# Selection products of the first layer in two PSUM banks by turns

## The chip, the cores and the metric

One core of a Trainium2 chip. The metric is device time in microseconds (us) of one execution; the kernel before takes 644.46 us, the median of 3 runs (644.11 to 645.67).

## What is computed

Two layers on x of 4 batches x 512 rows x 512 columns. Only the first layer is touched. Cut to it:

```python
xn = _layernorm(x, axis=-1)
s = einsum('bsk,nk->bsn', xn, w_masked) + bias            # 512 x 512 weight, masked by 32 x 32 blocks
inter = xn @ c1_w.T @ c2_w.T                              # rank 16, 1792 columns
idx = argmax(inter.reshape(rows, 56, 32), axis=-1) + arange(0, 1792, 32)
h = relu(einsum('bkm,bm->bk', w1[idx], xn))               # one of each 32 rows of w1 per row of x
g = silu(einsum('bk,bkm->bm', h, w2t[idx]))
x = x + s * g
```

The second layer (attention with one head, and a base weight with experts of low rank) follows on the same rows, with no edit in it.

## The kernel before

A chunk is one batch: 512 rows, in 4 tiles of 128 (`tt`). For each of the 4 chunks of the first layer the kernel computes all 1792 hidden values with dense products, and zeroes those that aren't the first largest of their 32. Products are made of a high and a low part of each operand, three matmuls for one.

The selection: `rank_product` (line 1192) makes the 16 rank values of a chunk in the bank `sel` (bank 6); ACT rounds them (`t_round`, L707) and the DVE takes the rest (`t_rest`, L926). Then for each piece `p` of 512 columns (4 pieces, the last of 256) and each tile `tt`, 16 in all, `select` on PE (L1214) writes 128 rows x 512 columns into `sel`. On the DVE `select_largest` takes the maximum of each 32 columns (`seg_top`, L939) and marks the places equal to it (`eq`, L941), both read out of the bank; `select_count` counts the marks within each 32 by a scan (`counts`, L953), which reads SBUF only. The counts are transposed, in the first chunk by PE (`first_transpose`, L1233, into bank 7), later by a DMA. Where the count is 1 the hidden value stays: `h` (L974). `h` is rounded on ACT (`h_hi`, L779), its rest taken on the DVE (`h_lo`, L983), and both go into the down product.

The order on each engine is written out by hand. On PE the head of a chunk is `rank_product`, then for each tile `s_product` (12 matmuls, L415) and `select(c, 0, tt)`. The body is a loop over 14 tiles `it` of hidden values: the up product of `it` (12 matmuls), the selection product of the next piece, and the down product of `it - 2` (12 matmuls), which waits for `h_lo`. In the first chunk the order is `up_product(0)`, `select(0, 0, 0)`, `up_product(1)`, then the four `s_product`s with `select(0, 0, 1)` to `select(0, 0, 3)` behind the first three; then `select(0, 1, 0)`, and `first_transpose(0)`, which waits for all four scans of piece 0.

The wait of a selection product is on the `eq` of the one before, since both use bank 6:

```python
                if p == 0 and tt == 0:
                    pe.wait_ge(t_split, c + 1)
                else:
                    pe.wait_ge(sel_eq, c * NSEL + p * TT + tt)
```

Each chunk of the DVE goes in the same order: in `body`, for `it` = 0, it does `h`, then `select_largest(c, 1, 0)`, then `h_lo`, then `select_count(c, 1, 0)`. ACT copies each `s_product` out of its bank (`s_read`, L713); in the first chunk it then rounds the next tiles of the weights (`w1_round`, `w2_round`, L723 and L728), and POOL subtracts (`w1_rest`, `w2_rest`, L614 and L619).

Of the kernel before, what the change touches and what calls it, by code (L numbers as in the profile page):

```python
# [18 lines left out]
def block_mask_ffn_then_attention_lora_kernel(  # L19
# [33 lines left out]
    SEG = 32  # L53
    KD = D // P
    TT = S // P
    CH = B
    PIECES = -(-INTER // BANK)
    PW = [min(BANK, INTER - p * BANK) for p in range(PIECES)]
# [17 lines left out]
    with ctx:  # L76
        def sem(name):
            return ctx.enter_context(nc.semaphore(name))
# [112 lines left out]
        t_stack = span_t.take("t_stack", [P, S], F32R)  # L191
# [18 lines left out]
        banks = [ctx.enter_context(nc.psum_tensor(f"bank{i}", [P, BANK], F32)) for i in range(8)]  # L210
# [57 lines left out]
        sel_eq = sem("sel_eq")  # L268
# [131 lines left out]
        def rows(tt):  # L400
            return slice(tt * P, (tt + 1) * P)

        def opens(c):

            return isinstance(c, int) and c == 0

        def s_bank(c, tt):

            return acc[tt] if isinstance(c, int) and c == 0 else up[tt % 2]

        def three(dst, pairs, start=True, stop=True):

            mms = [(a, b) for ah, al, bh, bl in pairs for a, b in ((ah, bh), (ah, bl), (al, bh))]
            for n, (a, b) in enumerate(mms):
                last = nc.tensor.matmul(dst, a, b, start=(start and n == 0), stop=(stop and n == len(mms) - 1))  # L415
            return last
# [7 lines left out]
        up = [banks[0], banks[1]]  # L424
        acc = [banks[2 + tt] for tt in range(TT)]
        sel = banks[6]
        mask_bank = banks[5]
        first_bank = banks[7][:].bitcast(BF16)[:, 0:S]
        first_counts = [counts, first[:, 1]]
        NSEL = PIECES * TT  # L430
# [450 lines left out]
        def _(dve):  # L881
# [47 lines left out]
            def select(c, p, tt):  # L929

                select_largest(c, p, tt)
                select_count(c, p, tt)

            def select_largest(c, p, tt):
                n = p * TT + tt
                segs = PW[p] // SEG
                got = sel[:, 0:PW[p]].rearrange("p (s n) -> p s n", n=SEG)
                dve.wait_ge(sel_done, c * NSEL + n + 1)
                nc.vector.reduce_max(seg_top[:, 0:segs], got, AX.X).then_inc(seg_max, 1)  # L939
                dve.wait_ge(seg_max, c * NSEL + n + 1)  # L940
                nc.vector.tensor_tensor(eq[:, 0:PW[p]].rearrange("p (s n) -> p s n", n=SEG), got,  # L941
                                        seg_top[:, 0:segs, None].to_broadcast([P, segs, SEG]),
                                        ALU.is_equal).then_inc(sel_eq, 1)
# [17 lines left out]
            def body(c, last):  # L961
                for it in range(IT):
                    if 0 < it < 4 * (PIECES - 1):
                        select(c, it // 4 + 1, it % 4)
                    dve.wait_ge(relu_done, c * IT + it + 1)
                    if opens(c):
                        dve.wait_ge(first_tr, it + 1)
                        which = first_bank
                    else:
                        if it % 4 == 0:  # L970
                            for tt in range(TT):
                                dve.wait_ge(ld_first[tt], (c * PIECES + it // 4 + 1) * 16)
                        which = first[:, it // 4 % 2, it % 4, :]
                    nc.vector.scalar_tensor_tensor(h[:], which, 1.0, h[:], ALU.is_equal, ALU.mult).then_inc(h_masked, 1)  # L974
                    if IT - 8 <= it < IT - 4:
                        rows_stats(dve, c + 1, it - (IT - 8))
                    if it == IT - 4:
                        dve.wait_ge(stats_in, (c + 1) * TT + TT)
                    if it == 0:

                        select_largest(c, 1, 0)
                    dve.wait_ge(h_hi_done, c * IT + it + 1)
                    nc.vector.tensor_tensor(h_lo[:, it % 2, :], h[:], h_hi[:, it % 2, :].bitcast(F32),  # L983
                                            ALU.subtract).then_inc(h_split, 1)
                    if it == 0:
                        select_count(c, 1, 0)
                    if it == IT - 4:
                        rows_moments()
                    if it == IT - 2:
                        rows_norm(dve, c + 1)  # L990
# [18 lines left out]
            for k in range(KD):  # L1009
                dve.wait_ge(ws_hi_done, k + 1)  # L1010
                nc.vector.tensor_tensor(ws_lo[:, k, :], ws_raw[:, k, :], ws_hi[:, k, :].bitcast(F32),
                                        ALU.subtract).then_inc(ws_split, 1)
            select_largest(0, 0, 0)
            c2_rest(1)
            select_count(0, 0, 0)
# [170 lines left out]
        def _(pe):  # L1186
# [9 lines left out]
            def s_product(c, tt, early=False):  # L1196

                if not early and tt >= 2:
                    pe.wait_ge(s0_read, c * TT + tt - 1)
                for k in range(KD):  # L1200
                    if early and tt == 0:
                        pe.wait_ge(ws_split, k + 1)
                    last = three(s_bank(c, tt)[:], [(xT_hi[:, k, rows(tt)], xT_lo[:, k, rows(tt)], ws_hi[:, k, :], ws_lo[:, k, :])],
                                 start=(k == 0), stop=(k == KD - 1))
                last.then_inc(s0_done, 1)

            def select(c, p, tt):


                if p == 0 and tt == 0:  # L1210
                    pe.wait_ge(t_split, c + 1)
                else:
                    pe.wait_ge(sel_eq, c * NSEL + p * TT + tt)
                nc.tensor.matmul(sel[:, 0:PW[p]], t_stack[:, rows(tt)],  # L1214
                                 c2_stack[:, p * BANK:p * BANK + PW[p]], start=True, stop=True).then_inc(sel_done, 1)

            def up_product(c, it, early=False):

                if it >= 2:
                    pe.wait_ge(relu_done, c * IT + it - 1)  # L1220
                elif not early:
                    pe.wait_ge(s0_read, c * TT + TT - 1 + it)
                pe.wait_ge(w1_lo, it + 1)
                three(up[it % 2][:], [(w1_hi_t[:, it, k, :], w1_lo_t[:, it, k, :], xT_hi[:, k, :], xT_lo[:, k, :])
                                      for k in range(KD)]).then_inc(up_done, 1)
# [10 lines left out]
            def down_product(it, tts):  # L1236

                pe.wait_ge(w2_lo, it + 1)
                for tt in tts:
                    last = three(acc[tt][:], [(h_hi[:, it % 2, rows(tt)], h_lo[:, it % 2, rows(tt)],  # L1240
                                               w2_hi_t[:, it, :], w2_lo_t[:, it, :])], start=(it == 0), stop=(it == IT - 1))
                return last

            def head(c):
                pe.wait_ge(xT_done, c * TT + TT)
                rank_product()
                for tt in range(TT):
                    s_product(c, tt)
                    select(c, 0, tt)

            def body(c, first):
                if not first:
                    up_product(c, 0)


                for it in range(1, IT + 1):
                    if it < IT:
                        if not (first and it == 1):
                            up_product(c, it)
                        if (it - 1) // 4 + 1 < PIECES:  # L1260
                            select(c, (it - 1) // 4 + 1, (it - 1) % 4)
                    else:
                        pe.wait_ge(relu_done, c * IT + IT - 1)
                        transpose_rows(pe, c + 1, 0)
                    if first:
                        first_transpose(it - 1)
                    if it >= 2:
                        pe.wait_ge(h_split, c * IT + it - 1)
                        if first and it == 2:
                            pe.wait_ge(s0_read, TT)  # L1270
                        down_product(it - 2, range(TT)).then_inc(down_done, 1)
                pe.wait_ge(relu_done, c * IT + IT)
                transpose_rows(pe, c + 1, 1)
                pe.wait_ge(xT_done, (c + 1) * TT + 1)
                transpose_rows(pe, c + 1, 2)
                pe.wait_ge(h_split, c * IT + IT)
                down_product(IT - 1, range(0, 2))
                pe.wait_ge(xT_done, (c + 1) * TT + 2)
                transpose_rows(pe, c + 1, 3)
                down_product(IT - 1, range(2, TT)).then_inc(down_done, 1)  # L1280
# [237 lines left out]
```

## Time and profile before

| what | value |
|---|---|
| median of 3 runs | 644.46 us (644.11 to 645.67) |
| profiled execution | 643.79 us, its span 642.0 us |
| PE busy | 627.1 us, 98% of the span |
| PE weight loads | 503.9 us, 78% |
| DVE busy | 443.0 us, 69% |
| ACT busy | 213.1 us, 33% |
| POOL busy | 245.1 us, 38% |

One execution is profiled; all rows below are of it, and the times in them count from the start of the span. A matmul of 512 columns is shown as 0.39 us long and the next starts about 0.23 us later, since they are pipelined. Line numbers are those of the kernel before. Busy shares are averages; the stalls and the chain are read from the timeline.

### The profile page before, as it was taken

To read this page: it belongs to the slowest core of one execution; us is meant where nothing else is said; L and a number is where in the kernel's file an instruction comes from. 1 tells how busy PE (TensorE), PEld (TensorE's weight loads), DVE (VectorE), ACT (ScalarE), POOL (GpSimd) and SP (SyncE) were. 2 spreads that over 40 slices of the span, in tenths; PEclk is the share of its full clock that TensorE was granted. 3 is DMA by queue.
4 is the path that set the end of the run, shared out by engine and by line. 5 is a ranking of instruction groups with operands and counts; after the bars stand their busy time and mean duration, and the time that the engine had idled before them with its cause. 6 is when DMAs were issued, how large, how long until landed. Compare 5 with 4: busy or idle time off the path is not lost.

```text
span 642.0 us, 8382 instructions
## 1 busy us (share of the span) xinstructions
PE 627.1 (98%) x2910; PEld 503.9 (78%) x2910; DVE 443.0 (69%) x706; ACT 213.1 (33%) x379; POOL 245.1 (38%) x184
## 2 busy tenths in 40 slices
PE   7999999999999999999999999999999999999997
PEld 3768787878888878888878887787877778787886
DVE  7987776687766786766787786676468447745654
ACT  3533432412222312222313243652245134414521
POOL 1455545560000560000550454477316530832353
PEclk9999999999999999999999999999999999999999
DMA  8950000021500021400052722271226034300701
GB/s 247 402 200 1 2 0 1 10 91 33 155 17 9 17 91 29 151 16 8 25 141 45 234 82 75 83 182 67 66 84 182 16 114 102 96 33 34 199 17 51
DMA packets 47311, 54.68 MB, mean 85 GB/s; under 512 B 25648, under 2 KB 26032, under 8 KB 46640
## 3 DMA queue, kind: packets, MB, share of 16 engines
q1 hardware_dynamic: 47280, 54.28, 28.2%
q8 instruction: 18, 0.29, 0.2%
q14 instruction: 13, 0.11, 0.1%
HBM read 40.24 MB, written 8.52 MB: 76 GB/s over the span
## 4 chain that ended last, share of the span: by engine, by line
PE 62%; issue 16%; DVE 11%; POOL 8%; ACT 1%; DMA 1%; POOLq 0%; DVEq 0%; ACTq 0%; SPq 0%
PE bank L415 56%; POOL prod_lo L692 4%; DVE counts L953 3%; POOL g_tile L391 2%; DVE seg_top L939 2%; PE bank L345 2%; POOL g_tile L395 2%; DVE eq L941 2%; PE bank L1214 1%; DMA first<-counts 1%; PE bank L1192 1%; DVE h_lo L983 1%; DVE h L974 1%; POOL rstd L379 1%; DVE ws_raw L1007 1%
## 5 line engine op out<-in xcount | busy, mean ns | idle before, releaser
L415 PE MATMUL bank<-w_hi_t,h_hi 128*128 128x512 f32 x224 | 90.3, 403 | 0.3
L779 ACT ACTIVATE h_hi<-h 128x512 fp32r<-128x512 f32 x56 | 35.4, 632 | 162.8 <-DVE h L974 162.8
L415 PE MATMUL bank<-w_lo_t,h_hi 128*128 128x512 f32 x224 | 87.6, 391 | 0.0
L415 PE MATMUL bank<-xT_hi,w_hi_t 128*128 128x512 f32 x224 | 87.3, 390 | 0.0
L415 PE MATMUL bank<-w_hi_t,h_lo 128*128 128x512 f32 x224 | 87.3, 390 | 0.0
L415 PE MATMUL bank<-xT_hi,w_lo_t 128*128 128x512 f32 x224 | 87.2, 389 | 0.0
L415 PE MATMUL bank<-xT_lo,w_hi_t 128*128 128x512 f32 x224 | 87.2, 389 | 0.0
L391 POOL TENSOR_TENSOR g_tile<-g_tile,s_tile 128x512 f32<-128x512 f32 x31 | 45.7, 1473 | 107.9 <-DVE g_tile L1103 57.3
L953 DVE TENSOR_TENSOR_SCAN counts<-restart,eq 128x512 bf16<-128x512 bf16 (+1 forms) x56 | 74.2, 1326 | 2.4
L939 DVE TENSOR_REDUCE seg_top<-bank 128x16 f32<-128x512 f32 (+1 forms) x64 | 39.5, 618 | 47.3 <-PE bank L1214 47.3
L692 POOL TENSOR_TENSOR prod_lo<-prod,prod_hi 128x512 fp32r<-128x512 f32 x32 | 51.2, 1636 | 31.5 <-ACT prod_hi L819 31.5
L377 POOL TENSOR_TENSOR rstd<-mean_var,eps 128x4 f32<-128x4 f32 x8 | 1.6, 203 | 152.7 <-DVE mean_var L371 152.7
L983 DVE TENSOR_TENSOR h_lo<-h,h_hi 128x512 fp32r<-128x512 f32 x56 | 41.2, 736 | 27.0 <-ACT h_hi L779 25.4
L415 PE MATMUL bank<-b_hi,prod_hi 128*128 128x512 f32 (+1 forms) x136 | 52.4, 385 | 2.0 <-POOL prod_lo L692 1.8
L758 ACT ACTIVATE h<-bank 128x512 f32<-128x512 f32 x56 | 33.5, 598 | 55.5 <-DVE h_lo L983 46.5
L415 PE MATMUL bank<-b_lo,prod_hi 128*128 128x512 f32 (+1 forms) x136 | 51.3, 377 | 0.0
L415 PE MATMUL bank<-b_hi,prod_lo 128*128 128x512 f32 (+1 forms) x136 | 51.3, 377 | 0.0
L415 PEld LDWEIGHTS bank<-w_hi_t,h_hi 128*128 128x128 f32 x224 | 42.1, 188 | 10.0 <-DVE h_lo L983 1.5
L415 PEld LDWEIGHTS bank<-w_hi_t,h_lo 128*128 128x128 f32 x224 | 42.1, 188 | 9.4
L415 PEld LDWEIGHTS bank<-xT_hi,w_lo_t 128*128 128x128 f32 x224 | 42.0, 188 | 8.8
L415 PEld LDWEIGHTS bank<-xT_lo,w_hi_t 128*128 128x128 f32 x224 | 42.1, 188 | 8.7
L415 PEld LDWEIGHTS bank<-xT_hi,w_hi_t 128*128 128x128 f32 x224 | 42.1, 188 | 8.7
(183 smaller groups left out, 1278.0 us busy)
## 6 DMA issues: line engine op xcount, KB each, us to landing
prod<-expert_weights SPq DMA_DIRECT2D x32, 256.0 KB, 5.6
w_raw<-in_w SPq DMA_DIRECT2D x28, 256.0 KB, 9.5
x_res<-in_x SPq DMA_DIRECT2D x4, 1024.0 KB, 8.5
mid_state<-g_tile SPq DMA_DIRECT2D x16, 256.0 KB, 2.1
x_tile<-mid_state SPq DMA_DIRECT2D x4, 1024.0 KB, 5.6
x_res<-mid_state SPq DMA_DIRECT2D x4, 1024.0 KB, 8.2
out<-g_tile SPq DMA_DIRECT2D x15, 256.0 KB, 2.0
x_tile<-in_x SPq DMA_DIRECT2D x3, 1024.0 KB, 5.8
```

Source lines behind the costliest of these rows:

```text
L345: last = nc.tensor.transpose(rows_bank(g, tt)[:, k * P:(k + 1) * P], x_tile[:, tt, k * P:(k + 1) * P], ident[:])
L379: nc.gpsimd.tensor_tensor(rstd[:], rstd[:], neg_half[:], ALU.pow).then_inc(rstd_step, 1)
L391: nc.gpsimd.tensor_tensor(g_tile[:, tt, :], g_tile[:, tt, :], s_tile[:, tt, :], ALU.mult).then_inc(s_free, 1)
L395: nc.gpsimd.tensor_tensor(g_tile[:, tt, :], g_tile[:, tt, :], x_res[:, tt, :], ALU.add).then_inc(rows_done, 1)
L415: last = nc.tensor.matmul(dst, a, b, start=(start and n == 0), stop=(stop and n == len(mms) - 1))
L692: nc.gpsimd.tensor_tensor(prod_lo[:, kt, :], prod[:, kt, :], prod_hi[:, kt, :].bitcast(F32), ALU.subtract).then_inc(prod_split, 1)
L758: nc.scalar.activation(h[:], up[it % 2][:], ACT.Relu).then_inc(relu_done, 1)
L779: nc.scalar.activation(h_hi[:, it % 2, :], h[:], ACT.Copy).then_inc(h_hi_done, 1)
L939: nc.vector.reduce_max(seg_top[:, 0:segs], got, AX.X).then_inc(seg_max, 1)
L941: nc.vector.tensor_tensor(eq[:, 0:PW[p]].rearrange("p (s n) -> p s n", n=SEG), got, seg_top[:, 0:segs, None].to_broadcast([P, segs, SEG]), ...
L953: nc.vector.tensor_tensor_scan(kept[:, tt, 0:PW[p]], restart[:, 0:PW[p]], eq[:, 0:PW[p]], 0.0, ALU.mult, ALU.add).then_inc(sel_count, 1)
L983: nc.vector.tensor_tensor(h_lo[:, it % 2, :], h[:], h_hi[:, it % 2, :].bitcast(F32), ALU.subtract).then_inc(h_split, 1)
```

## The change

The selection products of odd tiles go to bank 7 (`more_sel`), those of even tiles stay in bank 6. This holds for all pieces of chunks 1 to 3, and for piece 0 of chunk 0; in the later pieces of chunk 0 all stay in bank 6, since bank 7 then holds the transposed counts. `sel_bank` names the bank for PE and for the DVE. With two banks a product waits for the `eq` of the product before the last (`n - 1`), and the product `n` = 1 for none.

```diff
+        def sel_bank(c, p, tt):
+
+            return more_sel if tt % 2 and not (opens(c) and p) else sel
...
         sel = banks[6]
+        more_sel = banks[7]
...
             def select_largest(c, p, tt):
                 n = p * TT + tt
                 segs = PW[p] // SEG
-                got = sel[:, 0:PW[p]].rearrange("p (s n) -> p s n", n=SEG)
+                got = sel_bank(c, p, tt)[:, 0:PW[p]].rearrange("p (s n) -> p s n", n=SEG)
...
             def select(c, p, tt):
-                if p == 0 and tt == 0:
+                n = p * TT + tt
+                if n == 0:
                     pe.wait_ge(t_split, c + 1)
-                else:
-                    pe.wait_ge(sel_eq, c * NSEL + p * TT + tt)
-                nc.tensor.matmul(sel[:, 0:PW[p]], t_stack[:, rows(tt)],
+                elif opens(c) and p:
+                    pe.wait_ge(sel_eq, c * NSEL + n)
+                elif n > 1:
+                    pe.wait_ge(sel_eq, c * NSEL + n - 1)
+                nc.tensor.matmul(sel_bank(c, p, tt)[:, 0:PW[p]], t_stack[:, rows(tt)],
                                  c2_stack[:, p * BANK:p * BANK + PW[p]], start=True, stop=True).then_inc(sel_done, 1)
```

No instruction of PE or the DVE is moved against another. The places at which PE's bank or wait differ look like this one, the product of tile 3 in the opening of the first chunk, before:

```order
82 L415 MATMUL bank4<-ws_lo_83,xT_hi_75 128x512
83 L415 MATMUL bank4<-ws_hi_81,xT_lo_76 128x512
84 L1214 MATMUL bank6<-c2_stack_114,t_stack_115 128x512 [waits sel_eq]
85 L415 MATMUL bank5<-ws_hi_81,xT_hi_75 128x512
86 L415 MATMUL bank5<-ws_lo_83,xT_hi_75 128x512
```

and with the change:

```order
82 L419 MATMUL bank4<-ws_lo_83,xT_hi_75 128x512
83 L419 MATMUL bank4<-ws_hi_81,xT_lo_76 128x512
84 L1222 MATMUL bank7<-c2_stack_114,t_stack_115 128x512 [waits sel_eq]
85 L419 MATMUL bank5<-ws_hi_81,xT_hi_75 128x512
86 L419 MATMUL bank5<-ws_lo_83,xT_hi_75 128x512
```

The bank is another, the place between the `s_product`s is the same, and the count that `sel_eq` has to reach is lower by one.

## Rows read from the trace of the kernel before

**Rows 1.** The page: busy time by engine, and the chain by engine

```profile
PE 627.1 (98%) x2910; PEld 503.9 (78%) x2910; DVE 443.0 (69%) x706; ACT 213.1 (33%) x379; POOL 245.1 (38%) x184
...
PE 62%; issue 16%; DVE 11%; POOL 8%; ACT 1%; DMA 1%; POOLq 0%; DVEq 0%; ACTq 0%; SPq 0%
```

**Rows 2.** Line L1214, whom it waits for, who waits for it; then view of waits

```profile
  DVE eq L941: 9.0, 12
...
  DVE seg_top L939: 47.3, 46
...
PE bank L1214 <- DVE eq L941: 3.3, 6, 0.8
```

**Rows 3.** Timeline, opening of chunk 0: start us, us, engine line op, [idle before <-releaser]

```profile
23.57 0.40 PE L415 MATMUL bank<-ws_hi,xT_hi 128*128 128x512 f32 x1
...
26.10 0.39 PE L415 MATMUL bank<-ws_hi,xT_lo 128*128 128x512 f32 x1
26.54 0.50 PE L1214 MATMUL bank<-c_stack,t_stack 128*128 128x512 f32 x1
...
29.87 0.69 DVE L941 TENSOR_TENSOR eq<-bank,seg_top 128x512 bf16<-128x512 f32 x1
...
30.62 0.50 PE L1214 MATMUL bank<-c_stack,t_stack 128*128 128x512 f32 x1 [0.84 <-DVE eq L941]
...
36.86 0.39 PE L415 MATMUL bank<-ws_hi,xT_lo 128*128 128x512 f32 x1
37.29 0.60 ACT L713 ACTIVATE s_tile<-bank 128x512 f32<-128x512 f32 x1 [2.79 <-PE bank L415]
...
37.51 0.47 PE L1214 MATMUL bank<-c_stack,t_stack 128*128 128x512 f32 x1 [0.26 <-DVE eq L941]
...
38.67 0.40 PE L1233 MATMUL bank<-ident_bf,counts 128*128 128x128 bf16 x4 [0.70 <-DVE counts L953]
```

**Rows 4.** The chain that ended last, window 33 to 43 us: start, us, what

```profile
36.05 0.59 DVE seg_top L939
...
36.67 0.70 DVE eq L941
...
37.39 1.23 DVE counts L953
...
39.07 2.82 PE bank L415 x12
```

**Rows 5.** Timeline, head and start of the body of chunk 2

```profile
224.67 0.39 PE L1214 MATMUL bank<-c_stack,t_stack 128*128 128x512 f32 x1
...
236.00 0.39 PE L415 MATMUL bank<-xT_hi,w_lo_t 128*128 128x512 f32 x1
...
236.98 0.68 DVE L983 TENSOR_TENSOR h_lo<-h,h_hi 128x512 fp32r<-128x512 f32 x1
237.12 0.50 PE L1214 MATMUL bank<-c_stack,t_stack 128*128 128x512 f32 x1 [0.72 <-DVE eq L941]
...
237.71 0.50 PE L415 MATMUL bank<-w_hi_t,h_hi 128*128 128x512 f32 x1
```

**Rows 6.** Timeline, POOL and the scan on the DVE, 30 to 39 us

```profile
30.29 1.28 POOL L619 TENSOR_TENSOR w_lo_t<-w_raw,w_hi_t 128x512 fp32r<-128x512 f32 x1
30.60 2.05 DVE L953 TENSOR_TENSOR_SCAN counts<-restart,eq 128x512 bf16<-128x512 bf16 x1
...
31.53 2.20 POOL L614 TENSOR_TENSOR w_lo_t<-w_raw,w_hi_t 128x512 fp32r<-128x512 f32 x1
...
38.48 1.28 POOL L614 TENSOR_TENSOR w_lo_t<-w_raw,w_hi_t 128x512 fp32r<-128x512 f32 x1 [3.51 <-ACT w_hi_t L723]
```

**Rows 7.** Timeline of PE, start of the program: warming matmuls, then the first transposes

```profile
1.65 8.72 PE L1285 MATMUL bank<-restart 128*128 128x512 bf16 x28 [1.65 <-DVE restart L886]
...
6.74 3.62 PE L1285 MATMUL bank<-restart 128*128 128x512 bf16 x16
...
11.23 0.52 PE L345 MATMUL bank<-ident,x_tile 128*128 128x128 f32 x3 [0.87 <-DVE x_tile L385]
```

## The prediction

> **What bounds the kernel now.** I read the page first, for the engines and the chain [rows 1]. PE is busy 627.1 of 642.0 us and PE rows are 62% of the chain that ended last: only what lies in PE's own stalls, or moves PE's start, can change the time. The stalls that the diff speaks of are in the view of the selection's line [rows 2]: in front of the 64 products of `select` PE and its weight loads stand idle 9.0 us, 12 times, for the DVE's `eq`, and the view of waits puts 3.3 us of that, 6 times, on the matmul side. The other products find their wait met or nearly so. The same view says that the DVE waits for these products 46 times, 47.3 us; that is idle time of an engine that is busy 69%, and costs nothing by itself.
>
> A stall removed is a gain only where the next thing PE needs is not late as well, so each of the places is followed in the timeline. There are two kinds.
>
> **Place 1, the opening (26 to 39 us).** PE runs four products of the first weight, 12 matmuls each, with a selection product behind the first three [rows 3]. Its stalls show at 26.54 (the row before starts at 26.10 and the pace is 0.23, so 0.2 us), at 30.62 (0.84 idle) and a small one before the third; then come 37.51 (0.26) and the transposes at 38.67 (0.70, for `counts`). What they wait for is one chain on the DVE without a hole: the windowed chain of work [rows 4] goes maximum, `eq`, scan, each on the DVE and each right behind the one before, and only from 39.07 on is it mostly PE. So the DVE doesn't wait there for a selection product.
>
> **Place 2, the first two tiles of the next piece, once in each of the later three chunks.** The example is the third chunk [rows 5]. The product at 237.12 stood 0.72 idle for `eq`. The next matmul, at 237.71, belongs to the down product and waits for `h_lo`, which runs 236.98 to 237.66. This pair stands three times, with the same gap. In the head of a chunk the products come behind 12 matmuls each and find `eq` finished, as the one at 224.67, with no idle time in its row.
>
> **The change, part by part.**
>
> *Bank and waits.* No instruction is added, and the order on PE and DVE stays. Odd tiles write and are read from bank 7; reads of a bank cost the same by anything that I see (the DVE's maximum and `eq` come out of PSUM either way). One wait per chunk goes, that of the product `n` = 1; the others ask for one `eq` less: tiles 2 and 3 in the opening, and all from the second chunk on. The 12 selection products of the later pieces of the first chunk keep bank 6 and their wait, since bank 7 holds the transposed counts there. One of them, the product at 37.51, still waits for the `eq` of 36.67.
>
> *Waits that were met.* Heads and bodies of chunks 2 to 4: 48 products less the 3 of place 2. Nothing: PE's order puts them behind 12 or 24 other matmuls.
>
> *Place 2, 3 stalls.* The up product issues its last matmul at 236.00, so the selection product can go at 236.23, 0.89 earlier. But the down product still needs `h_lo`, whose DVE chain (`h`, maximum, `eq`, `h_lo`) contains nothing that waits for this product. It starts at 237.71 as before. 3 x 0 = 0. The cover is `h_lo`; without it each stall would return up to 237.71 - 236.46 = 1.25 us at most, and that is the bound for the range.
>
> *Place 1, PE.* From 23.57 on PE now runs without a stop: 4 x 12 matmuls and 3 selection products, so the last one starts 50 steps later. The step is (26.10 - 23.57) / 11 = 0.23, which gives 35.07 instead of 36.86 [rows 3]: 1.79 us earlier. The two waits that are left there are met: the second selection (about 29.3) needs the `eq` that had ended when 26.54 began, the third (about 32.3) the one of 29.87 + 0.69 = 30.56 [rows 3]. Then PE stands before the product at 37.51, since the `eq` of 36.67 ends when it did, and before the transposes, which want all four scans. So the 1.79 us turn into one longer wait, worth 0.
>
> *Place 1, what the earlier PE triggers.* The last copy out of PSUM on ACT (37.29) waits for PE; behind it on ACT stands the rounding of the next weight, and behind that POOL's subtraction at 38.48 [rows 3, 6]. All move 1.79 earlier: the copy to 35.50, POOL to 36.69. It then runs to 36.69 + 1.28 = 37.97, and lies across 37.39, where the DVE wants to start its fourth scan. The rows show what that costs [rows 6]: a scan that starts inside a POOL operation is stretched until 1.08 us after that operation's end: POOL 30.29 + 1.28 = 31.57, the scan of 30.60 ends at 32.65. The POOL operation behind it is stretched in its turn (31.53, 2.20 instead of 1.28). The fourth scan ran alone, in 1.22: 37.39 to 38.61 [rows 4]. Changed it ends at 37.97 + 1.08 = 39.05, 0.44 later. PE's transposes wait for it (0.70 of idle time at 38.67), and from there PE is the chain without a hole: [rows 4] shows the 12 matmuls at 39.07, and PE holds the chain in the same way for the rest of the chunk, 11 stretches of 24 matmuls. So **0.44 us are added**.
> The Trainium skill (GPSIMD Engine Reference, section 1, Specifications) says that GpSimd shares its SBUF interfaces with VectorE, with contention for DVE instructions with two SBUF inputs. The scan has two, and the rows above agree.
>
> *Sum.* 0 + 0 + 0.44 = 0.44 on the profiled execution of 643.79 us (span 642.0), so 644.2. That execution is 0.67 below the median, and the forecast for the median is 644.46 + 0.44, about **644.9 us**. Bounds of the unknown terms: the scan loses nothing if POOL comes after 37.39 (0), and almost a whole POOL operation if POOL starts just before it, 1.28 - (1.22 - 1.08) = 1.14. Place 2 lies between -3 x 1.25 and 0; I take 0, since `h_lo` is measured as the last.
>
> **Rivals.**
>
> *A: no effect at all* (20%). POOL is not early enough, or takes its turn in another way; then the time is 644.5. Against: 0.7 us of margin between 36.69 and 37.39.
>
> *B: the removed stalls are worth their time* (3%). If PE's stalls were on the path, 1.79 in the opening and 3 x 0.6 (237.71 - 237.12 for the selection product that fills the gap) would return, 3.6 us: 640.9, faster by 0.6%. For it speaks the 9.0 us of idle time; against it, that in both places another DVE result ends after the stall.
>
> *C: PE's clock falls in the longer hole* (4%). Waits that were spread are put together: PE would be idle from about 35.3 to 37.51, runs one product, and is idle again to 39.1. Of the 28 warming matmuls at the start of the program the first 12 took 6.74 - 1.65 = 5.09 us and the last 16 took 3.62 [rows 7]; with 0.2 taken off for the last one's own end that is 0.42 against 0.21 each, so I read the first as run at the lower of the two levels, 1.2 GHz. All took 8.72, where 28 x 0.214 + 0.2 = 6.2 would do: a spell at the lower level costs 2.5 us. With the 0.44 this gives 647.4, slower by 0.46%. It decides if the hole is long enough for the throttle. Against: the matmuls kept the upper pace over holes of 0.87 [rows 7] and 0.84 us [rows 3], though these are shorter than 2.2.
> The Trainium skill (TensorE: Matmul & The Clock Gate, Part 1) says that the gate halves the clock after idle time; by it the hole would cost those 2.5 us if it counts as idle. No row of this trace has a hole so long.
>
> *D: POOL gets two turns before the scan* (4%). The scan would wait for the second subtraction as well, 1.28 more: 646.2. Against: the POOL operation at 31.53 waited behind the scan that was already due [rows 6].
>
> *E: the change does not act*, because a wait for the old bank survives. The order of PE shows bank 7 and the missing wait, so this has no chance of its own beyond A.
>
> **The numbers.** Forecast 69%, A 20%, B 3%, C 4%, D 4%. Forecast and A lie within 0.3%, about what a measurement of this kernel can tell from no change (1.9 us, 642.5 to 646.4); so does D. Same 0.93, slower 0.04, faster 0.03. The three runs before spread over 644.11 to 645.67, and the median may move with them. The range takes A from below (644.5 less 0.5), the bound of the scan (644.46 + 1.14), and half a microsecond of spread: 644.0 to 646.1, which leaves out B, C and a part of D.
>
> **What the profile afterwards would show.** Right: the first four selection products at about 20.6, 26.3, 29.3 and 32.3; the last matmul of the fourth product at 35.1; POOL's subtraction near 36.7; the fourth scan about 1.66 long; PE's transposes at about 39.1; in the later chunks the product about 0.9 before its old place and the down product exactly on it. Wrong: a fourth scan of 1.22 (A), transposes before 38.6 or a down product that starts earlier after `h_lo` (B), matmuls of the first up product paced at over 0.4 us (C).

## The result, and the profile after

The changed kernel takes 648.23 us, the median of 6 runs (646.91 to 649.05), against 644.83 us (644.11 to 645.67, 6 runs) for the kernel before, measured together. The ratio is 1.0049, with a 95% interval of 1.0035 to 1.0063: slower by half a per cent, outside the predicted range of 644.0 to 646.1. It is the case that the prediction called C. All six runs have a mean granted clock of TensorE of 0.992 to 0.996. The profiled execution took 649.05 us, its span is 647.2.

The page of the changed kernel, busy times, the granted clock in 40 slices, and the chain by engine:

```profile
PE 629.5 (97%) x2910; PEld 507.0 (78%) x2910; DVE 445.8 (69%) x706; ACT 213.1 (33%) x379; POOL 244.1 (38%) x184
...
PEclk9979999999999999999999999999999999999999
...
PE 61%; issue 16%; DVE 12%; POOL 8%; ACT 1%; DMA 1%; POOLq 0%; DVEq 0%; ACTq 0%; SPq 0%
```

Against [rows 1] the shares hardly move, and a reader of the busy times would see nothing. One digit of the clock says where to look: slice 3 of 40, 32 to 48 us. The changed kernel's stretches there (us, PE busy and count, granted clock, DMA share, GB/s):

```profile
36.00:37.00 1.00, 0.00 (x0) 1.00 1.06 408
37.00:38.00 1.00, 0.66 (x1) 0.65 1.05 408
38.00:39.00 1.00, 0.08 (x1) 0.50 1.05 410
...
43.00:44.00 1.00, 1.00 (x4) 0.50 0.00 0
44.00:45.00 1.00, 1.00 (x8) 0.94 0.00 0
```

The clock falls from its upper level (2.4 GHz) to 0.50 of it (1.2 GHz) and comes back at about 44.1. The row of 37 to 38 us, 0.65, puts the fall at 37.3: 0.3 us at the upper level and 0.7 at the lower. PE's timeline over the same place, which answers to [rows 3]:

```profile
34.90 0.39 PE L419 MATMUL bank<-ws_hi,xT_lo 128*128 128x512 f32 x1
37.18 0.66 PE L1222 MATMUL bank<-c_stack,t_stack 128*128 128x512 f32 x1 [1.89 <-DVE eq L946]
38.92 0.61 PE L1241 MATMUL bank<-ident_bf,counts 128*128 128x128 bf16 x4 [1.09 <-DVE counts L958]
...
39.87 0.63 PE L419 MATMUL bank<-xT_lo,w_hi_t 128*128 128x512 f32 x1
40.29 0.63 PE L419 MATMUL bank<-xT_hi,w_lo_t 128*128 128x512 f32 x1
```

PE got through the opening as forecast, then had nothing for 1.89 us, one product, and nothing for 1.09. I call such idle time a hole, and a stretch at the lower level a spell. The clock fell 0.1 us into that one product, so behind the first hole and before the second. From the product on the matmuls take longer, and behind the second hole they start every 0.42 us instead of 0.23. The DVE, ACT and POOL beside it, which answer to [rows 4, 6]:

```profile
35.33 0.60 ACT L718 ACTIVATE s_tile<-bank 128x512 f32<-128x512 f32 x1 [2.35 <-PE bank L419]
...
36.52 1.27 POOL L619 TENSOR_TENSOR w_lo_t<-w_raw,w_hi_t 128x512 fp32r<-128x512 f32 x1 [1.88 <-ACT w_hi_t L728]
...
37.06 1.80 DVE L958 TENSOR_TENSOR_SCAN counts<-restart,eq 128x512 bf16<-128x512 bf16 x1
```

The fourth scan is 1.80 us instead of 1.22: POOL ends at 37.79, and the scan 1.07 later. A second spell stands in the head of the third chunk. The chain of the changed kernel, in order of time (start, us, what):

```profile
121.11 2.12 PE bank L1197 x8
...
144.62 5.73 PE bank L419 x24
...
216.76 2.12 PE bank L1197 x8
...
241.29 7.38 PE bank L419 x24
...
338.60 5.74 PE bank L419 x24
```

24 matmuls take 7.38 us at 241.29, and 5.73 in the second and last chunks; the granted clock falls there at 242.1, 0.8 us behind the hole. PE's timeline in front of it, and the scan in that head that made its hole longer:

```profile
238.90 0.39 PE L1222 MATMUL bank<-c_stack,t_stack 128*128 128x512 f32 x1
241.29 0.50 PE L419 MATMUL bank<-w_hi_t,h_hi 128*128 128x512 f32 x1 [2.00 <-DVE h_lo L988]
...
223.42 2.37 DVE L958 TENSOR_TENSOR_SCAN counts<-restart,eq 128x512 bf16<-128x512 bf16 x1
223.42 1.29 POOL L391 TENSOR_TENSOR g_tile<-g_tile,s_tile 128x512 f32<-128x512 f32 x1
```

In the kernel before, the same two rows were these; the scan began 0.03 us ahead of POOL, and POOL was the one stretched:

```profile
220.75 1.22 DVE L953 TENSOR_TENSOR_SCAN counts<-restart,eq 128x512 bf16<-128x512 bf16 x1
220.78 2.28 POOL L391 TENSOR_TENSOR g_tile<-g_tile,s_tile 128x512 f32<-128x512 f32 x1
```

The account of the 5.2 us between the two profiled spans closes on four terms, read at the start of each chunk's rank product (before: 118.47, 214.11, 309.80; after: 121.11, 216.76, 314.99) and at PE's transposes and down products:

| term | us |
|---|---|
| fourth scan longer, 1.80 - 1.22 (the DVE's chain itself began 0.33 earlier in this run) | 0.58 - 0.33 = 0.25 |
| transposes to second rank product, 82.19 against 79.80: first spell | 2.39 |
| third head, rank to down product, 24.53 against 23.60: met scan | 0.93 |
| down product to last rank product, 73.70 against 72.09: second spell | 1.61 |
| sum | 5.18 |

The first and third rows together are 1.2, the two spells 4.0. The profiled run is the slowest of the six; how the 3.4 us between the medians divide in the other five isn't shown. The third row is not of the change: it is a race that one or the other kernel can lose. `open_only` below, whose later chunks are as before, lost it as well (2.36 us, a head of 24.52). But there the old waits split PE's idle time in front of the down product, and the clock stayed at 1.00.

### The profile page after: what moved, and what is told of

The parts are those of the page before. It is cut to its first block, busy times and chain, and to the rows that moved or that the text cites. A ratio compares the mean times of both kernels' runs of the same rounds, so it can differ in the third digit from the quotient of the medians.

```text
span 647.2 us, 8380 instructions
## 1 busy us (share of the span) xinstructions
PE 629.5 (97%) x2910; PEld 507.0 (78%) x2910; DVE 445.8 (69%) x706; ACT 213.1 (33%) x379; POOL 244.1 (38%) x184
## 4 chain that ended last, share of the span: by engine, by line
PE 61%; issue 16%; DVE 12%; POOL 8%; ACT 1%; DMA 1%; POOLq 0%; DVEq 0%; ACTq 0%; SPq 0%
PE bank L419 56%; POOL prod_lo L697 4%; DVE counts L958 3%; POOL g_tile L391 2%; DVE seg_top L944 2%; DVE eq L946 2%; POOL g_tile L395 2%; PE bank L345 1%; PE bank L1222 1%; DMA first<-counts 1%; PE bank L1197 1%; DVE h_lo L988 1%; DVE h L979 1%; POOL rstd L379 1%; PE bank L1241 1%
## 5 line engine op out<-in xcount | busy, mean ns | idle before, releaser
L391 POOL TENSOR_TENSOR g_tile<-g_tile,s_tile 128x512 f32<-128x512 f32 x31 | 43.7, 1411 | 108.0 <-DVE g_tile L1108 57.4
L958 DVE TENSOR_TENSOR_SCAN counts<-restart,eq 128x512 bf16<-128x512 bf16 (+1 forms) x56 | 75.6, 1350 | 2.4
```

The source lines that it names most:

```text
L391: nc.gpsimd.tensor_tensor(g_tile[:, tt, :], g_tile[:, tt, :], s_tile[:, tt, :], ALU.mult).then_inc(s_free, 1)
L958: nc.vector.tensor_tensor_scan(kept[:, tt, 0:PW[p]], restart[:, 0:PW[p]], eq[:, 0:PW[p]], 0.0, ALU.mult, ALU.add).then_inc(sel_count, 1)
```

## The experiments

Theory 1 from here on: the change doesn't make PE wait less, it puts PE's idle time together, and the clock falls there; the stretched scan is a small second term. The rivals are that the later chunks carry the loss, that the second bank costs something by itself, and that POOL and the scan are the whole of it. "Clock" below is the mean granted clock of a run; it doesn't say where a spell was. In the 111 runs of the kernel before that were made beside these experiments it was 0.996 twice and never lower, and 0.997 or less in 15. The edits are shown against the changed kernel; those of versions with one bank are the same against the kernel before.

**The opening alone.** Only piece 0 of the first chunk uses two banks.

```diff
-            return more_sel if tt % 2 and not (opens(c) and p) else sel
+            return more_sel if tt % 2 and opens(c) and not p else sel
...
-                elif opens(c) and p:
+                elif p or not opens(c):
```

> Only piece 0 of the first chunk uses two banks; the later chunks are as before. Theory 1 (the hole of PE in the opening, 2.3 us and then 1.5 us with one product between, takes the granted clock down to its lower level, and a scan meets a POOL operation): slower by nearly all of the whole change, 2.5 to 3.5 us, the first up product behind the hole shown at 0.50 of the clock in most runs. Theory 2 (the later chunks carry it): within 0.5 us of before.

648.15 us (644.98 to 650.46, 4 runs) against 644.49; ratio 1.0066 (1.0045 to 1.0086). Three runs have a clock of 0.991 or 0.992 and take 647.7 to 650.5. The fourth, 0.998, takes 645.0, and it is the profiled one: its fourth scan is 1.79 us, its holes are 1.90 and 1.26 us, its clock stays at 1.00 all the same, and its first down product starts as early as in a kernel without a spell (42.40, for 42.17 and the 0.25 of the scan). The opening carries the loss, and in most runs the clock is low, not in all. The slowest run is 6.0 us over before, more than one spell of 2.4 us; what else it had isn't shown.

**The later chunks alone.**

```diff
-            return more_sel if tt % 2 and not (opens(c) and p) else sel
+            return more_sel if tt % 2 and not opens(c) else sel
...
-                elif opens(c) and p:
+                elif opens(c):
```

> Only the later chunks use two banks; the opening is as before. Theory 1: within 0.5 us of before, with now and then a spell of lower clock in one head (1.7 us, as the third chunk of the changed kernel shows). Theory 2: slower by 1.7 us or more in most runs.

645.44 us (644.13 to 648.93, 10 runs); ratio 1.0016 (1.0000 to 1.0033). Eight of the ten lie at 644.1 to 646.2; the other two have clocks of 0.994 and 0.995 and take 648.9 and 647.2. In the profiled run, 646.0, the third head again has a scan of 2.34 us, a hole of 1.98 us in front of the down product, and 24 matmuls in 7.36 us. So heads have spells now and then: a smaller, rarer part.

**Two banks, old waits.**

```diff
-                elif opens(c) and p:
+                else:
                     pe.wait_ge(sel_eq, c * NSEL + n)
-                elif n > 1:
-                    pe.wait_ge(sel_eq, c * NSEL + n - 1)
```

> The two banks, with the waits of the kernel before. Theory 1 (only when PE runs matters): the kernel before, within 0.5 us, granted clock 1.0 in the opening. Rival (reading or writing the second bank costs something by itself): slower by 1 us or more, with longer maxima or eq on the DVE.

644.45 us (643.60 to 644.60, 10 runs), ratio 0.9993 (0.9983 to 1.0003). The bank costs nothing that can be measured. Of the change only the lower counts in the waits are left as a cause, that is, when PE runs.

**PE kept busy in the opening's holes**, by matmuls whose result nobody reads.

```diff
+                        if first and it == 1:
+                            pe.wait_ge(relu_done, 1)
+                            fill(up[0], 8)
                         if (it - 1) // 4 + 1 < PIECES:
                             select(c, (it - 1) // 4 + 1, (it - 1) % 4)
+                        if first and it == 1:
+                            fill(up[0], 6)
```

> The changed kernel with 8 matmuls without use in front of, and 6 behind, the selection product at 37 us, into bank 0, so that PE is busy through the hole. Theory 1: the clock stays at 1.0 in the opening; what is left over before is the stretched fourth scan, 0.3 to 0.5 us, and spells in the heads of some runs, so 0.3 to 1.5 us over before instead of 3.4. If the loss comes from the scan and POOL alone: no change against the changed kernel.

647.41 us (646.50 to 649.48, 5 runs); ratio 1.0046 (1.0029 to 1.0064). The clock stays at 1.00 in the opening as expected, but the time is 2.9 over before, more than I allowed. The profiled run, 647.41, has its loss in the last chunk, where the DVE waited 4.34 us for the transposes by DMA and PE stood 2.85 us. Stretches of it (as above):

```profile
335.00:338.00 3.00, 2.50 (x6) 0.55 0.76 294
338.00:340.00 2.00, 2.00 (x9) 0.82 0.25 57
```

So one can have a clean opening and lose in a head. Of this run's 3.6 us, 1.8 are the head that ended later (the down product 25.36 us behind the rank product, for 23.59), and 1.5 the spell (24 matmuls in 7.21 us for 5.74). The late transposes are thus a loss of their own, and another run, with a clock of 1.0, takes 646.50: 2.0 us over before, with no spell to be seen. Why this version loses that, and why the next one, with the same 14 matmuls in the opening, doesn't, stays open.

**PE kept busy in every hole**: as before, and 5 such matmuls (`fill(acc[0], 5)`) behind the second selection product of the next piece in each later chunk.

> The changed kernel with matmuls without use in every hole that it makes: 8 and 6 about the product at 37 us, and 5 behind the second selection product of the next piece in each later chunk. Theory 1 (spells of lower clock behind the holes are most of the loss, and heads too have them where a scan lost the race against POOL): mean granted clock 0.999 or more in nearly all runs, and 0.5 to 1.0 us over before. Rival (the loss in the heads is POOL's and the scans' alone): no better than the kernel with the opening filled, 2.5 us over before.

645.42 us (644.16 to 646.20, 10 runs) against 644.73; ratio 1.0006 (0.9996 to 1.0016). Clocks 0.999 or 1.0 in nine of ten. What is left over before, 0.7 us in the medians, is about the stretched fourth scan (1.73 us in its profile, 0.5 more than alone), but the interval doesn't tell it from nothing. The 29 matmuls without use, 14 in the opening and 5 in each of three later chunks, take away the loss of the change: the loss was PE's idleness, not its work.

**Only the first hole of the opening left empty** (`fill(up[0], 0)` in place of 8).

> As fill_all, but the first hole of the opening (35.1 to 37.1 us, the one that the change makes) is left empty; behind the product at 37 us 6 matmuls run. If the spell needs the long run of idleness with only one product in it: no spell, as fill_all. If the 2 us alone are enough: clock at 0.50 behind it, 2 to 3 us over fill_all in most runs.

645.33 us (644.07 to 648.01, 10 runs); ratio 1.0014 (0.9996 to 1.0033). Seven runs lie at 644.1 to 646.5; the others are 646.9, 647.9 and 648.0, with clocks of 0.997, 0.995 and 0.997. The profiled run, 644.5, has a hole of 1.90 us at 37.41 and no spell. So with only the first hole left the clock is low (0.997 or less) in three runs of ten, and with both in three of four of `open_only` and in all six of the changed kernel, though these have unfilled heads as well. The second hole thus counts in some runs; but in the profiled run of the changed kernel the clock fell before it, and how it counts isn't shown.

**The stretched scan taken away, the hole left.** One more wait on POOL in the opening:

```diff
+                if it == 4:
+                    gp.wait_ge(sel_count, TT)
```

> The changed kernel with one wait more on POOL: its subtraction that met the fourth scan waits for that scan. The scan is 1.22 us again and PE's transposes 0.6 us earlier. If the spell of lower clock in the opening comes from the hole that the change makes (35.1 to 37.1 us) and the one behind it, now 1.3 instead of 1.9 us: fewer spells, 1 to 3 us over before in the runs that have them and within 0.3 us in the rest. If the scan's 0.6 us were the whole price: before, within 0.3 us, in every run.

645.74 us (644.07 to 649.06, 10 runs) against 643.92; ratio 1.0033 (1.0015 to 1.0051). The fourth scan is 1.22 us. The run with a clock of 1.0 takes 644.07, which is the kernel before; the six from 0.990 to 0.996 take 645.7 to 649.1, and the three of 0.997 take 645.1 to 645.6. The two terms are apart: the scan 0.6 us, the spells the rest. In the profiled run the holes are 2.00 and 0.70 us, and the clock falls at about 39.4, behind the second, for a shorter time:

```profile
38.00:40.00 2.00, 1.30 (x9) 0.86 0.96 374
40.00:42.00 2.00, 2.00 (x6) 0.50 0.17 65
42.00:44.00 2.00, 2.00 (x11) 0.79 0.00 0
```

**Can the holes themselves go?** What makes them is a DVE chain whose scans meet POOL. First try, on both kernels: in the opening POOL's subtractions after the fourth scan, in the later heads the bias additions after the fourth scan.

```diff
-            gp.wait_ge(c2_split, 2)
-            for it in range(2, IT + 2):
+            gp.wait_ge(ws_split, KD)
+            w1_rest(2)
+            gp.wait_ge(sel_count, TT)
+            w2_rest(0)
+            for it in range(3, IT + 2):
...
             def head(c):
+                if not opens(c):
+                    gp.wait_ge(sel_count, c * NSEL + TT)
```

> The kernel before (one bank), with POOL's subtractions of the opening moved off the first four scans and its bias additions behind the fourth scan of each later head. If a scan that starts inside a POOL operation loses what the rows show (0.83 us each) and the DVE's chain sets PE's start there: the opening is 1.7 us shorter (two scans), each of three heads 0.85 (one scan), 642.2 to 640.2 in all, faster by 2.3 to 4.3 us. If something else holds PE: no change.

> The same on the changed kernel (two banks). PE's hole in the opening shrinks from 2 + 1.5 us to about 0.6 + 1.1 and in the heads from 1.25 to 0.4, so theory 1 expects no spells of lower clock and the same time as the one-bank version within 0.5 us. If the two banks cost something apart from the holes: slower than the one-bank version by over 1 us.

Not faster, either of them: 646.18 us (ratio 1.0010, 0.9998 to 1.0021) and 646.14 (1.0016, 1.0002 to 1.0031), against 644.73. The opening did get shorter, PE's transposes are at 36.91 (one bank) instead of 38.67. But POOL's queue was now behind, and met the scans of the next piece and `h_lo`, which reads two tensors of SBUF as well. The chain of the one-bank version:

```profile
43.63 0.04 DVE first L958
43.67 1.95 issue
45.62 0.67 DVE h L979
...
46.98 1.58 DVE h_lo L988
...
48.61 7.32 PE bank L415 x24
```

The first two scans of the next piece, at 39.98 and 43.63, take 2.31 and 2.07 us instead of 1.22 (the second lies under the 1.95 us of "issue" in this view), `h_lo` takes 1.58 instead of 0.69, and PE's hole behind it, 1.79 us, brings a spell with one bank too: 7.32 us for 24 matmuls, for 5.55 before. The two-bank version has the same hole of 1.79 us there and no spell in its profile. So a spell comes behind a hole, whatever makes it, and not each time.

**POOL between the scans.** While the DVE does the maximum and `eq` out of PSUM (1.4 us), a POOL operation of 1.3 us fits.

```diff
-            gp.wait_ge(c2_split, 2)
-            for it in range(2, IT + 2):
+            gp.wait_ge(ws_split, KD)
+            w1_rest(2)
+            gp.wait_ge(sel_count, 1)
+            w2_rest(0)
+            gp.wait_ge(sel_count, 2)
+            w1_rest(3)
+            gp.wait_ge(sel_count, 3)
+            w2_rest(1)
+            gp.wait_ge(sel_count, 4)
+            for it in range(4, IT + 2):
```

> The kernel before (one bank) with POOL's four subtractions of the opening put between the scans, where the DVE reads PSUM (one behind the high and low parts of the first weight, three each behind a scan). The scans are 1.22 us instead of 2.05: transposes at 37.0 instead of 38.7, and unlike with the late subtractions no queue behind them, so faster by 1.4 to 1.7 us. If POOL's work is late for the first chunk again: no gain.

> The changed kernel with POOL's four subtractions of the opening between the scans. PE's hole in the opening is then 0.6 + 1.1 us at most, the heads keep their whole hole behind the selection product (1.25 us, 2.1 where the first scan lost against POOL). Theory 1 (the clock falls where the change puts idle time together): no spell in the opening; spells left in the heads, so between the one-bank version of the same (642.7) and 1.7 us over it. Rival (the opening is all): 642.7 within 0.3.

One bank: 642.71 us against 643.92, ratio 0.9984 (0.9975 to 0.9994). Two banks: 642.28 against 644.01, ratio 0.9982 (0.9968 to 0.9996), seven of ten runs within 641.8 to 642.6 and three of 642.9 to 645.4. All opening scans are 1.22 us. With two banks the opening has no spell in the profiled run, and its lowest run is 0.7 us under the one-bank kernel's (641.82 for 642.52), which I had not expected; the medians are 0.4 apart. The DVE's row for the first `h_lo` tells why, one bank first:

```profile
39.11 1.70 DVE L991 TENSOR_TENSOR h_lo<-h,h_hi 128x512 fp32r<-128x512 f32 x1
```

and two banks:

```profile
39.62 0.68 DVE L996 TENSOR_TENSOR h_lo<-h,h_hi 128x512 fp32r<-128x512 f32 x1
```

The earlier PE lets POOL start its first subtraction at 37.17 instead of 37.73, and the second at 38.41 instead of 38.98. With two banks the second one ends at 39.71, just behind the start of `h_lo`; with one it runs until 40.27, and `h_lo`, which starts at 39.11, is stretched by it. From the transposes to the first down product PE takes 4.23 us with one bank and 3.49 with two. The same lead that lost a scan before wins an `h_lo` here.

**POOL's rows of the heads between the scans too.** `gate` gets `pace`, the number of the next chunk's first selection product, for each chunk but the last of the layer. First the bias additions go in two pairs (the second pair behind the first scan of the next piece):

```diff
+            if pace is not None and tt >= 2:
+                gp.wait_ge(sel_count, pace + 2 * tt - 3)
...
+            if pace is not None and tt >= 2:
+                gp.wait_ge(sel_count, pace + 2 * tt - 2)
...
+                    if tt == 2 and not opens(c):
+                        gp.wait_ge(sel_count, c * NSEL + TT + 1)
```

> The same, and in the heads of the later chunks POOL's last four operations on the rows each wait for a scan, and two of the four bias additions for the first scan of the next piece. All scans 1.22 us; the down product of each head 0.9 to 1.2 us earlier than 23.6 behind the rank product, and the runs in which the first scan loses against POOL (0.9 us more) gone: 4 to 5.5 us faster than before, and a spread under 1 us.

> The same POOL order with two banks (the change). With no long wait of PE left to put together, no spells of lower clock: within 0.5 us of the one-bank version. If it is slower by over 1 us, two banks cost something that the holes don't explain.

644.67 us (ratio 1.0010, 1.0000 to 1.0020) and 644.29 (1.0007, 0.9997 to 1.0016). The head is 23.0 us instead of 23.6, from rank product to down product, and all its scans are 1.22. It is given back at once: the body behind it takes 73.2 us to the next rank product instead of 72.1. The first pair of additions meets `h` in the head (1.82 us), and the second pair meets the second scan of the next piece in the body (2.34).

**All four bias additions behind the second `h_lo`**: the wait, in front of the four and in place of the one between the pairs, is `gp.wait_ge(h_split, c * IT + 2)`.

> One bank. POOL's work of the opening between the scans, the last four operations of each head on the rows each behind a scan, and all four bias additions behind the second h_lo of the chunk, where the body of the chunk has room. The slotted version before it won 0.6 us in each head and lost 1.1 to bias additions that met the h and the second scan; without these the head is 22.4 to 22.7 instead of 23.6 and nothing is given back: 639 to 641. If the additions meet something else on the way: as slots_one, 644.5.

> The same with two banks. The waits that the change removes are then hidden nearly everywhere and PE has no hole of 2 us: theory 1 expects no spell, and the one-bank version within 0.4 us. If spells of lower clock came with two banks as such: slower by 1 us or more in some runs, mean granted clock under 0.998.

642.68 us (0.9982, 0.9972 to 0.9992) and 641.94 (0.9965, 0.9953 to 0.9976). The head is now 22.35 us, PE has no hole of 0.8 us or more in it, but the four additions in a row, 6.39 us, meet the third tile. The DVE of the one-bank version:

```profile
242.32 1.60 DVE L967 TENSOR_TENSOR_SCAN counts<-restart,eq 128x512 bf16<-128x512 bf16 x1
243.84 1.71 DVE L988 SCALAR_TENSOR_TENSOR h<-first,h 128x512 f32<-128x512 bf16 x1
246.25 1.00 DVE L997 TENSOR_TENSOR h_lo<-h,h_hi 128x512 fp32r<-128x512 f32 x1 [0.70 <-ACT h_hi L793]
```

The profiled run of the two-bank version, 643.0 with a clock of 0.997, is 1.1 us over its median, and its spell stands before the first place that the change touches, at 26 us: PE waited 1.94 us for the first tile of x, until 11.87, and the clock was at 0.50 from 12.7 to 16.1. So a clock a little under 1.0 can also be a spell of the start of the program; the other six runs have 0.999 or 1.0.

**One addition behind each `h_lo`**, from the second tile on: `gp.wait_ge(h_split, c * IT + 2 + tt)` inside the loop.

> As paced_one (one bank), but the four bias additions of a chunk go one by one, each behind the h_lo of one tile from the second on, where the DVE next reads PSUM. In paced_one each head won 1.25 us and gave 1.0 back where the four additions in a row met the scan, h and h_lo of the third tile. If that was it: 1.0 us less in each of three chunks, 639.7 instead of 642.7. If the additions meet the DVE at each step anyway: no change.

> The same with two banks: 3 us under paced_two, 638.9, and no spell of lower clock. The two banks against one: 0.7 us faster, as in the opening of the two versions before; if the difference is more or less than 0.3 to 1.1, it has a source outside the opening.

639.62 us (639.38 to 640.41, 4 runs) against 644.44, ratio 0.9926 (0.9909 to 0.9944), and 638.63 us (638.55 to 638.87, 4 runs), ratio 0.9909 (0.9893 to 0.9926). Nothing is given back. The chain of the two-bank version in the third chunk is PE alone:

```profile
233.27 5.44 PE bank L423 x24
238.71 0.23 PE bank L1236
238.93 5.44 PE bank L423 x24
```

This is the best kernel of the study, 5.8 us under the kernel before, and it holds the change. Two banks are 1.0 us better than one here, and no run of one version reaches into the other's. All of it comes from the opening: the first down product is at 40.12 instead of 41.20, while from the second rank product to the third both take 94.34 us.

## Why the prediction was wrong

- **What bounds the kernel.** Right: only PE's stalls count, and in both places another result of the DVE is later than the `eq` that the change no longer waits for. The stalls in front of the `select` line all but went (one left on the matmul side, 1.89 us, for 3.3 us in 6), and no time came with them. `later_only`, which has the later chunks' part alone, is not faster than before.
- **Place 1, PE.** Right: the last matmul of the fourth product was forecast for 35.07 and came at 34.90, the selection products at 26.29, 29.24 and 32.18.
- **Place 1, the earlier POOL and the scan.** The mechanism was right and the size a little low: 0.58 us (a scan of 1.80) for the 0.44 of the sum. POOL stood at 36.52, 0.5 us ahead of the scan. `fill_all`, without the spells, is 0.7 us over before, which fits this term but doesn't measure it.
- **Place 2.** Right in the profiled second and last chunks: the down product stands 23.51 and 23.61 behind the rank product, as before. Wrong as a rule: the term was put at 3 x 0, and its bound had only gains in it. In the third chunk the same idle time in one piece cost a spell of 1.6 us.
- **The step that failed is the one that turned the 1.79 us of place 1 "into one longer wait, worth 0", with 4% for rival C against it.** The longer wait was not free. C's mechanism, its place and its price are what happened: 2.39 us for a spell in the opening where C had 2.5, and all six runs had a clock under 0.997. The same spell in the third head, 1.61 us, was in no term at all. Between 26 and 40 us PE was idle for 2.0 us before (14 less 12.0 busy), in four pieces, and for 3.0 us now (14 less 11.0), in two; the idle time didn't go, it moved together. The argument against C was that the clock had held over 0.84 and 0.87 us. But the hole was forecast at 2.2, and no row showed that the clock bears such a hole, or that it doesn't; 4% was much too sure, and the range should have taken in C's 647.4.
- **The Trainium skill's rule** (TensorE: Matmul & The Clock Gate, Part 1), that the gate halves the clock after idle time, was cited as what would make C true. The trace agrees: 0.50 from 37.3 us on, behind 1.89 us of idleness. It also fell behind 1.98 and 2.00 us of idleness in heads.
- **Rival B** (the stalls are worth their time) is out: `old_waits` has them and is no slower than the versions of the same group without them, and the run of `open_only` without a spell, where the opening's are gone, takes 645.0. **Rival D** (two POOL turns before the scan) didn't happen. Rival A (no effect) is none of the six runs.
- **Missed altogether**: the heads have a race. The first scan and a POOL operation start within 0.03 us of each other, and the loser is 0.9 us later. The scan loses it in 5 of the 13 profiled runs in which POOL's operations on the rows don't wait for a scan, each time in the third chunk, and two of these five (`open_only`, `late_pool_one`) have the old waits in the heads. With the changed waits the hole there is 2.00 us in this kernel and 1.98 in `later_only`, and both have a spell behind it. How often the kernel before loses it was not measured.

## What to carry to other kernels

Before a wait is taken off the engine that bounds, ask where its idle time goes: if the next thing that it needs comes no earlier, the same idleness stands in one piece, and a TensorE hole of 2 us may cost more than it lasts. A hole whose length the sum can tell, and which is longer than every one that the trace shows, deserves an even chance of a fallen clock, unless work fills it: in the profiles here the clock fell behind 7 holes of 14 between 1.6 and 2.9 us. The cure that paid was on the engines that made the hole: each POOL operation put where the DVE reads PSUM, one at a time, since a queue of them only moves the collision.

## What the runs showed of the hardware

- In the 19 profiles TensorE stood idle 14 times for 1.6 to 2.9 us after it had begun work. The granted clock fell to 0.50 in or behind 7 of them: 1.79 (`late_pool_one`), 1.89 and 2.00 (the change), 1.94 (`paced_two`), 1.98 (`later_only`), 2.00 (`no_meet`) and 2.85 us (`fill_open`). It held at 1.00 behind the other 7: 1.63 (`slots_open_two`), 1.79 (`late_pool_two`), 1.85 (`no_meet`), 1.90 (`open_only`, `fill_second`), 2.08 (`spread_two`) and 2.21 us (`late_pool_one`). So the length alone doesn't decide at 2 us. In the 8 profiles without such a hole, with holes up to 1.49 us, it didn't fall while PE had work. The price of a spell was 2.39 us in the opening of the change, and 1.5 to 1.8 in its third head and in `later_only`, `fill_open` and `late_pool_one`.
- A scan, `h` or `h_lo` on the DVE and a `tensor_tensor` on POOL hold each other up. A scan that starts second ends about 1.08 us after POOL's operation, and POOL's second operation as much after a scan (220.78 + 2.28 against 220.75 + 1.22); `h` and `h_lo` end about 0.55 us after it (39.11 + 1.70 against 38.98 + 1.29). The second one was 0.3 to 1.2 us late. Started in the same 10 ns, the scan was the loser (2.37 us for 1.22). The maximum and `eq`, which read PSUM, ran beside POOL at their full 0.69. The Trainium skill (GPSIMD Engine Reference, section 1, Specifications) names this contention, for DVE instructions with two SBUF inputs; the measured rows agree.
- 29 matmuls without use in the holes held the mean clock at 0.999 or more in nine runs of ten, and the time at 1.0006 of before (0.9996 to 1.0016). 14 in the opening alone held the clock there in the profiled run, but that version was 2.9 us over before.
